# A gather by matmul with the operands exchanged: the table stationary, the one-hot moving

## What is computed

```
e = ln(mlp(edge_feat))                                  # 64 features for each edge
for s in range(2):
    ce = concat([e, n[senders], n[receivers]])          # 192 features for each edge
    e  = e + ln(mlp(ce, edge_blk[s]))                   # silu(ce @ w0 + b0) @ w1 + b1, then layer norm
    agg = segment_sum(e, receivers)
    n  = n + ln(mlp(concat([n, agg]), node_blk[s]))
```

## Time and profile before

| | us |
|---|---|
| median of 3 runs | 20097.11 (20082.25 to 20124.14) |
| the profiled execution's own time | 20072.68 |
| its span in the profile | 20070.7 |
| TensorE busy (matmul) | 15562.4 |
| VectorE busy | 13897.1 |
| ScalarE busy | 8145.1 |
| first edge-network pass, about | 8132 to 13713 |
| second edge-network pass, about | 14126 to 17712 |

### The profile page before, as it was taken

One profiled execution on the slowest core, in us unless ns is written; L12 is line 12 of the kernel. 1 busy time (PEld: TensorE's weight loads), 2 busy tenths in 40 slices (PEclk: granted clock), 3 DMA queues, 4 the chain that ended last, 5 costly groups with the idle time before them and its releaser, 6 DMA issues. The chain is left out here.

```text
span 20070.7 us, 577236 instructions
## 1 busy us (share of the span) xinstructions
PE 15562.4 (78%) x211534; PEld 14106.5 (70%) x211534; DVE 13897.1 (69%) x33414; ACT 8145.1 (41%) x17256; POOL 5737.8 (29%) x4543
## 2 busy tenths in 40 slices
PE   2666666666667996799999999996788888856665
PEld 1666666666654996788888888885677777746665
DVE  3777777777766996554555555554777777769999
ACT  0444444444442332455555555553344444421111
POOL 1888888888870110011111111110000000001111
PEclk9555555555556997899999999997899999977676
DMA  2222222222222552444444444442444444417676
GB/s 56 54 53 53 53 53 51 52 53 53 53 51 78 157 157 73 103 111 108 110 110 108 110 110 110 109 110 65 132 132 135 134 136 131 134 56 209 176 207 182
DMA packets 1403272, 2071.03 MB, mean 103 GB/s; under 512 B 764952, under 2 KB 938022, under 8 KB 1359282
## 3 DMA queue, kind: packets, MB, share of 16 engines
q1 hardware_dynamic: 1089098, 1709.41, 27.3%
q0 software_dynamic: 218240, 197.29, 8.9%
q10 hardware_dynamic: 94544, 142.53, 1.9%
HBM read 1521.71 MB, written 523.16 MB: 102 GB/s over the span
## 5 line engine op out<-in xcount | busy, mean ns | idle before, releaser
L759 POOL DMA_INDIRECT records<-e_sort_rec,e_sort_index x3300 | 4353.2, 1319 | 1064.0 <-issue 990.8
L2275 PE MATMUL e_s_ps_g<-e_s_parts,e_s_pick 128*128 128x64 bf16 x65340 | 2927.7, 200 | 760.4 <-DVE e_s_to_hot L1922 289.1
L2275 PEld LDWEIGHTS e_s_ps_g<-e_s_parts,e_s_pick 128*128 128x128 bf16 x65340 | 2679.7, 103 | 912.0 <-issue 599.7
L2280 PE MATMUL e_s_ps_g<-e_s_window,e_s_to_hot 128*128 128x64 bf16 x23100 | 1982.1, 199 | 25.8 <-issue 25.3
L1938 DVE COPY e_s_g_sb<-e_s_ps_g 128x512 f32<-128x512 f32 x880 | 605.7, 688 | 1847.8 <-PE e_s_ps_h L2298 1376.8
L2394 POOL DMA_DIRECT2D states<-e_s_second_t x550 | 475.0, 864 | 4919.1 <-ACT e_s_second_t L2134 4575.6
L1088 PE MATMUL e_sort_acc<-e_sort_thirds,e_sort_hot 128*128 128x48 f32 x7260 | 1574.7, 414 | 319.0 <-DVE e_sort_hot L918 319.0
L1088 PEld LDWEIGHTS e_sort_acc<-e_sort_thirds,e_sort_hot 128*128 128x128 f32 x7260 | 1557.0, 332 | 351.4 <-DVE e_sort_hot L918 351.4
L2385 POOL DMA_INDIRECT e_s_spill<-send,e_s_lists x220 | 243.5, 1107 | 4315.5 <-DMA e_s_window_in<-recv 4210.1
L2280 PEld LDWEIGHTS e_s_ps_g<-e_s_window,e_s_to_hot 128*128 128x128 bf16 x23100 | 1274.8, 102 | 28.4 <-issue 27.6
L1921 DVE TENSOR_SCALAR e_s_pick<-e_s_rows,lane_below 128x1024 bf16<-128x1024 bf16 (+1 forms) x3300 | 1243.2, 432 | 0.0
(11 more groups left out here) (540 smaller groups left out, 35769.6 us busy)
## 6 DMA issues: line engine op xcount, KB each, us to landing
e_s_rows<-rows_d SPq DMA_DIRECT2D x330, 1088.0 KB, 5.3
e_s_hot<-hots_d SPq DMA_DIRECT2D x550, 560.0 KB, 4.0
e_s_to_rows<-rows_d SPq DMA_DIRECT2D x220, 608.0 KB, 5.8
e_s_rows<-rows_d SPq DMA_DIRECT2D x220, 544.0 KB, 4.3
e_s_rows<-rows_d SPq DMA_DIRECT2D x220, 512.0 KB, 5.0
e_s_to_rows<-rows_d SPq DMA_DIRECT2D x220, 512.0 KB, 6.2
states<-e_s_first_t ACTq DMA_DIRECT2D x440, 256.0 KB, 2.5
states<-e_s_second_t POOLq DMA_DIRECT2D x440, 256.0 KB
```

The source lines that it names most:

```text
L759: pool.indirect_dma_start(records, bass.IndirectOffsetOnAxis(ap=index[x][:, t:t + 1], axis=0), rec[x][:, t, :], None,).then_inc(written[x] ...
L2275: pe.matmul(to_, pick[p][:, h, here], parts[:, SPAN * c + h, r, :], start=h == 0 and r == 0, stop=False)
L2280: mm = pe.matmul(to_, to_hot[p][:, here], window[:, r, 1, :], start=c == SPILL and r == 0, stop=r == 2)
```

## The change

In both passes `gather` loads the table part as the stationary operand, 128 rows by 64 columns, and moves the one-hot, 128 columns for each cell. The product comes out with features on partitions, in the form of the bank `ps_h1`, so it is accumulated there at once. The first cell of a pair goes to partitions 0 to 63 and the second to 64 to 127, and the loop alternates between these halves. For the receiver's window one matmul of up to 512 columns serves all cells of a half. `gathered_`, `g_sb`, `ps_g` and the transposes are gone; the spill rows are added in `hidden1` by a float32 product with the identity, which now waits for their DMA. `ps_h1` has 2 banks in the first pass and 5 in the second. `hidden1` moves one group earlier and, in TensorE's order, behind `hidden0`; `out1` moves one group earlier. ScalarE's `act1_` and `out1_` move with them; in the first pass `act1_` stands behind `act0_`, and `widens` behind `second_`. The spill DMA waits for `hidden1` of two blocks back in place of the copy.

```diff
+        NH = 2 if enc else 5
-        vg = chain(shared("mlp_gathered_v"), [f"{g}" for g in G_ALL] + ["spill"])
-        g_sb, act1 = tiles("g_sb", [LANES, 8 * D]), tiles("act1", [LANES, 512])
+        act1 = tiles("act1", [LANES, 512])
-        ps_g, ps_h1, ps_o1, ps_sum = ps("g", NB), ps("h1", NB), ps("o1", NB), ps("sum")[0]
+        ps_h1, ps_o1, ps_sum = ps("h1", NH), ps("o1", NB), ps("sum")[0]
+
+        def hidden_bank(x, s):
+            return ps_h1[(x + s) % 2 if enc else s]
-            def gathered_(k, x, s, before):
...
@@ vector body
-                    if main and s:
-                        gathered_(k - 1, y, s - 1, before - 1)
...
-                if main:
-                    gathered_(k - 1, y, 4, before - 1)
@@ scalar body, for s in range(NG + 3)
-                    if enc and out_ and s < NG:
-                        widens(k - 2, x, s)
...
                     if new and s < NG:
                         act0_(k, x, s, before)
+                    if enc and main and 1 <= s < NG + 1:
+                        act1_(k - 1, y, s - 1, before - 1)
                     if out_ and enc and 1 <= s < NG + 1:
                         second_(k - 2, x, s - 1, before - 2)
+                    if enc and out_ and s < NG:
+                        widens(k - 2, x, s)
                     if new and 1 <= s < NG + 1:
                         out0_(k, x, s - 1, before)
+                    if not enc and main and 1 <= s < NG + 1:
+                        act1_(k - 1, y, s - 1, before - 1)
                     if main and 2 <= s < NG + 2:
-                        act1_(k - 1, y, s - 2, before - 1)
-                    if main and s >= 3:
-                        out1_(k - 1, y, s - 3, before - 1)
+                        out1_(k - 1, y, s - 2, before - 1)
@@ tensor: gather
+                halves = [hidden_bank(x, s)[half * D:(half + 1) * D, :] for half in range(2)]
                 pe.wait_ge(vp.sem, vp.at(f"to{s}", k))
                 if s == 0:
                     pe.wait_ge(vx.sem, vx.end(k))
+                if s >= NH or before:
+                    pe.wait_ge(aH.sem, group_at(aH, "", k, s, NH))
+                to_pairs = to_hot[p][:, :].rearrange("p (j w l) -> p w j l", w=2, l=LANES)
+                for r in range(3):
+                    for half in range(2):
+                        n_ = (e - c0 + 1 - half) // 2
+                        pe.matmul(halves[half][:, 0:n_ * LANES], window[:, r, 1, :], to_pairs[:, half, 0:n_, :], start=r == 0, stop=False,
+                                  skip_group_check=True)
+                for j in pairs(s):
+                    mine = [(half, c0 + 2 * j + half) for half in range(2) if c0 + 2 * j + half < OWN]
+                    for h in range(SPAN):
+                        for r in range(3):
+                            for half, c in mine:
+                                mm = pe.matmul(halves[half][:, j * LANES:(j + 1) * LANES], parts[:, SPAN * c + h, r, :],
+                                               pick[p][:, h, (c - c0) * LANES:(c - c0 + 1) * LANES], start=False, stop=False, skip_group_check=True)
+                if e > OWN:
+                    j, half = divmod(OWN - c0, 2)
...
@@ tensor: hidden1
+                if s == NG - 1:
+                    j, half = divmod(SPILL - c0, 2)
+                    pe.wait_ge(spilled[x], block_of(k, x, 16))
+                    pe.matmul(hidden_bank(x, s)[half * D:(half + 1) * D, j * LANES:(j + 1) * LANES], spill[x][:, :], ident128[:, :], start=False, stop=False,
+                              skip_group_check=True)
-                pe.wait_ge(vg.sem, vg.at(f"{s}", k) if s < NG - 1 else vg.end(k))
-                if s >= NB or before:
-                    pe.wait_ge(aH.sem, group_at(aH, "", k, s, NB))
-                for j in pairs(s):
...
@@ tensor body, for s in range(NG + 3)
                     if new and s < NG:
                         hidden0(k, x, s, before)
+                    if main and 1 <= s < NG + 1:
+                        hidden1(k - 1, y, s - 1, before - 1)
...
                     if main and 2 <= s < NG + 2:
-                        hidden1(k - 1, y, s - 2, before - 1)
-                    if main and s >= 3:
-                        out1(k - 1, y, s - 3, before - 1)
+                        out1(k - 1, y, s - 2, before - 1)
@@ gpsimd: spill_
-                    pool.wait_ge(vg.sem, vg.end(k - 2))
+                    pool.wait_ge(tH.sem, tH.end(k - 2))
```

38 lines of the change are left out of this document (6 added, 32 removed).

## The result

The changed kernel takes 19951.56 us (median of 4 runs, 19924.17 to 19958.93), the one before 20098.17 (4 runs, 20082.25 to 20124.14): ratio 0.9921, 95% interval 0.9906 to 0.9935. The forecast was 19977, its reason a sum of 0 in the first pass and -1.1 us a block in the second. The profiled span went from 20070.7 to 19957.2 us.

What follows compares the result with a forecast made beforehand. It took the first pass as TensorE's, the second as shared with VectorE. First pass 0 (+0.5 path, -0.5 clock), second -1.1 us a block: -120 us from 20072.7 gives 19953, plus 24 for the median 19977; range 19500 to 20800.

Steps and rivals of the forecast that it cites:

- The gather, 29 ns a matmul: Gather, both passes: paired matmuls in the two column halves run side by side, a group 2.75 us against 2.81.
- One at a time: Rival, gather: halves do not overlap, 56 ns a matmul, 11.3 us a block more, 21200 us; chance 0.14.
- 42 ns: Rival, gather: load and stream of one half follow each other but halves overlap, 560 us more, 20500; chance 0.12.
- A drain at each change of shape: Rival, TensorE: changing tiling mode drains the engine, 0.17 us, ten a block, 1.7 in both passes, +300, 20270; chance 0.05.
- path +0.5: First pass, `first_` 0 to end of `out0` 4: removed wait and transposes against moved-in work and a new 1.5 us wait.
- wait 3.3: First pass: TensorE waits 3.3 us a block for VectorE's `norm0` before `first_` of group 0, 7.7 of 11.05 being filled.
- The clock, -0.5: First pass: loss from TensorE's time at 1.2 GHz falls from 1.5 to 1.0 us a block (0 to 1.7).
- Second pass, -1.1: Second pass: period falls 1.1 us a block (-0.3 to -2.5), -120 us, along the loop through roots, gather and VectorE's tail.
- Path +0.1: Second pass, `gather` 2 to the split: transposes -1.3, `gather` 4 +0.3, one more `out1` 1.1, in us a block.
- one copy ahead of `picks` 2, 0.6: Second pass, VectorE: removing one copy before `picks` 2 saves 0.6 us a block.
- I take a fifth off them, and a little off the time at 1.2 GHz: 0.6: Second pass: TensorE's instruction waits, 2.1 us a block, shrink by a fifth; with the clock, 0.6 saved.
- TensorE's work alone: Rival, both passes: chains have more slack, TensorE's work sets the pace, 8.5 us a block saved, 19050; chance 0.07.

Runs made afterwards that it cites:

- three small reorderings: Changed kernel; first pass: window and picks before group 4's variance, its `hidden1` behind `second_` and `sums`; second: group 0's picks before group 3's residual; 19550.3 us.
- runs of nine: Changed kernel with all nine pick matmuls of one half before its partner's nine, window's three likewise, both passes; 20229.7 us.
- runs of 39: Changed kernel with all 39 gather matmuls of one half before the other half's 39 in each group, both passes; 21454 us.

## Why the prediction was right, and where it was right for the wrong reason

- **The gather, 29 ns a matmul: right.** 28.1 measured, group 2.78 against 2.75. One at a time was a true alternative with the right price: 56 ns, 5.23 us a group, 21454 us, when the order of the loops was changed. That a load needs another row group to overlap, which the forecast cited from the Trainium skill ("TensorE: Matmul & The Clock Gate", Part 3) and which stood nearest to 42 ns, is not what this chip did: all loads and matmuls here use all 128 rows, and pairs go at 56 ns. The same part's other rule, that different column groups run at once, held.
- **A drain at each change of shape: not nothing, and nearly of the rival's size.** From the last full f32 product to the first window matmul the starts are 203 ns apart where they were 109 before the change, and from the last pick to the next full product 149 where a pair takes 56 (records at the 2.4 GHz level, first pass). Behind both stands a little more: the second pair of window products comes 240 ns after the first where 216 is usual, and the second full product 213 ns after the first where it was 193 (first pass) or 533 where such products are 432 apart (second pass). That is about 0.23 and 0.28 us a group, and the spill's product, with 64 columns between full ones, adds a change in and a change out: about 1.4 us a block in the first pass and 1.7 in the second, part of it inside waits, against that rival's 1.7. The forecast put 0. Its evidence was a 64-column transpose that is followed on time, and transposes do pass free here; but in the same trace the products of `hidden0` with 24 rows start 123 ns behind the gather's last matmul where full ones start 29 behind it, and the next full product 201 ns behind them where 112 is usual. The Trainium skill's rule on tiling modes ("TensorEngine Tiling (Array Packing)", Key Properties) fits it in kind.
- **First pass, path +0.5 and wait 3.3: right in kind, the size in part by luck.** `out0` of group 4 ends at 10020.67 + 0.61, and the next `first_` starts at 10032.62: 11.34 (11.05 forecast). The remaining path is 51.32 - 11.34 = 40.0 (40.2). The wait for `norm0` was 1.75, not 3.3, because TensorE's work ended later in the gap than counted:

```profile
10020.67 0.61 PE L2227 MATMUL e_s_ps_o<-w_eenc,e_s_act 128*128 128x128 f32 x4
...
10023.07 0.28 PE L2298 MATMUL e_s_ps_o<-row_eblk,ones 128*128 128x256 bf16 x1 [0.69 <-ACT e_s_unit L2140]
...
10025.09 0.55 PE L2206 MATMUL e_s_ps_h<-ident,e_s_lists 128*128 128x128 f32 x3 [0.26 <-issue]
...
10028.19 1.48 PE L2269 MATMUL e_s_ps_h<-e_s_pick,e_s_parts 128*64 128x128 bf16 x46 [1.06 <-issue]
```

From 10023.07 to the wait are 7.7 us where 5.9 were counted: in this block 1.3 of waiting for instructions and 0.2 of the switches. Over all blocks the mean is 7.7 too, with 0.65 of such waiting; the rest isn't parted. This moved the length of the wait, not the period. The new wait for `first_t` was 1.5 at group 4 as written. The period went up by 0.6, within -1.0 to +0.7. The path of 40.0 holds four groups' switches, about 0.9, which the forecast's 40.2 did not count; the shorter pitch (28.1 for 29 ns, some 230 matmuls) gives 0.2 of it back, and what gave the rest is not shown.
- **The clock, -0.5: not found, and this is the term that puts the first pass at 0 instead of +0.6.** Time that TensorE worked at the 1.2 GHz level, summed by me over the records, went from 2.8 to 2.4 us a block in the first pass, and half of that is the loss, 1.4 to 1.2. But other profiles give 2.95 for the code of before and 2.2 to 3.0 for that of after, so even this -0.2 is within the scatter.
- **Second pass, -1.1: the right loop, one of its terms too small by more than half.** The measured -1.78 is within -0.3 to -2.5, and the loop along which the sum was made is the one that the trace shows. "Path +0.1" and "one copy ahead of `picks` 2, 0.6" make -0.5 together; blocks in the same state give 0.0 to -0.4. The step that failed is "I take a fifth off them, and a little off the time at 1.2 GHz: 0.6". The waits for instructions went entirely (2.1 a block), the time at 1.2 GHz fell from 4.3 to 1.5, and together they are worth 1.4 to 1.7. That the sum stayed so near is in part luck: the copy and the path were taken for slightly more than they brought, this term for much less.
- **Why the instruction waits went is open.** Shorter turns are enough to end the fetches (26 are left). With the fetches back, at most 0.8 of the 2.1 us came back, so the length of the turn is not the whole reason.
- **"TensorE's work alone", 19050:** no. But its size was the right order for what could be had: three small reorderings, two of them at waits that the forecast named itself, gave 401 us more.

## What to carry to other kernels

Work taken off an engine is worth what the next wait leaves of it: after such a change, list the waits again, and reorder the queues of the other engines, which here brought 2.0% where the change itself had brought 0.8%. Don't take an engine's balance for a cause: 5.8 us a block left VectorE's queue, the balance closed to 0.1, and blocks in the same state were 0.0 to 0.4 us shorter. Follow the ring through all engines, and compare blocks with the same clock and the same instruction waits. And where two halves of the array can work side by side, alternate them instruction by instruction; the order of a loop was worth 7.5% here.

## What the runs showed of the hardware

- Two matmuls of 128 columns with 64-column tables in different column halves, each with its own load, start 3 to 8 ns apart and take 56 ns together; two in the same half are 56 ns apart.
- TensorE starts matmuls of one half ahead of earlier ones of the other half: with runs of nine, the starts are 6, 50, 30 and 26 ns apart around each change of half, and with runs of 39 the second half's first window matmul starts (10010.13) before the last three picks of the first.
- A change between the half-width tables and full-width products costs about 0.09 us to the next start, each way, and up to 0.1 more behind it; 64-column transposes between full ones cost nothing (109 ns a start throughout), products of 24 rows about 0.09 each way (123 for 29 ns, 201 for 112).
- After a wait of 3.1 us for VectorE the next gather, 2.78 us at full clock, took 4.26 to 4.43 us in all 109 blocks of a run; where the wait was 2.1 on average, it was over 3.5 in 39 of 106.
- A turn of 1744 of TensorE's records ran with 26 instruction fetches in 3390 us, the longer ones (2044 and more) with 438 to 458 in 3000 us, and these need not cost any time: 1.2 us of waiting in the best case, about 200 in the kernel before.
